# Root of the second layer's first norm: ScalarE's square root and VectorE's reciprocal, or one power on GpSimd

## The chip, the cores and the metric

The kernel runs on one core of a Trainium2 chip. The metric is the device time of one execution in microseconds (us), from the first to the last instruction with what lies around them; the median of the runs is what is compared. Engines are named as in the profile: PE (TensorE; PEld its weight loads), DVE (VectorE), ACT (ScalarE), POOL (GpSimd), SP (the queue that issues most transfers).

## The reference, cut to what matters

A two-layer model over 16 sequences of 548 tokens (36 from image patches, 512 from a word table) of 64 channels. The first layer is an attention with ReLU and a top-1 mixture of 8 experts with limited places; the second is a linear attention over 16 heads and a top-2 mixture of 8 experts. The part at stake is the norm ahead of the second layer's attention:

```python
def _layernorm(x, axis=-1, eps=1e-05):
    m = jnp.mean(x, axis=axis, keepdims=True)
    v = jnp.var(x, axis=axis, keepdims=True)
    return (x - m) / jnp.sqrt(v + eps)
...
h = h + _L0_ffn_ref(_layernorm(h, axis=-1), ...)      # first layer's experts
h = h + _L1_attn_ref(_layernorm(h, axis=-1), ...)     # the norm that is changed
h = h + _L1_ffn_ref(_layernorm(h, axis=-1), ...)      # second layer's experts
```

## The kernel before, in words

A sequence ("block" b, 0 to 15) is held as 128 partitions x 5 slots x 64 channels in `H[:, b]`. The kernel has two phases. Phase one runs the first layer for all blocks up to the scatter of the tokens to their experts, and then the first layer's experts in 24 units. Phase two, the functions `pool_second`, `pe_second`, `act_second` and `dve_second`, takes each block through: fetching the expert outputs (`gather_first`, 3 indirect transfers, and `gather_rest`, 2, both issued by POOL, L382), weighting and cleaning them (`scale`, `limits`, `mask`; on DVE inside `mixed` for the first BY_DVE = 3 blocks, on POOL from block 3 on), adding them to H (`mixed`, L650 and L652), the norm's statistics (`mixed_stats`: five `bn_stats` of L1354 and five `bn_aggr` of L1357), the root (`roots4`, ACT, L548), the norm itself (`norm4`, DVE, L670 to L673), PE's turn of it (`t4`, L977), ACT's copy of that (`stack4`, L566), keys and values (`kv`, L990), their bias (`kv_b`, DVE, L680), the norm of keys and values (`square`, `sum_squares`, `roots_kv`, `kvnorm`), the small products `gram` to `by_proj` (L447 to L472), `proj` (L990), its GELU on ACT (`gelu_proj`, L578), the second residual and its statistics (`resid2`, `resid2_stats`), two roots (`roots5`, L559 and L560), `norm5`, `route` (L496) and the choice of two experts. In that choice `second_share` (POOL, L412) raises a 128x5 tile of Euler numbers to a power. Then come the second layer's experts: for each block 8 units of two `up` halves (PE, L1012 and L1013), two GELUs (ACT, L607), a `down` (PE, L521), a `weigh` (DVE, L852) and a `summed` (POOL, L422).

Each engine runs its instructions in order. The order is set by hand: every function has a time in a table (`POOL_TWO`, `PE_TWO`, `ACT_TWO`, `DVE_TWO`), block b's is 32 later for each block, and `in_order` sorts each engine's list by these times. Engines are tied together by semaphores alone, so a function that waits holds all that stands behind it on its engine. On DVE the order around the norm is `mixed` 43, `mixed_stats` 45, `norm4` 67; `mixed` of the next block (75) comes after `norm4` of this one. On POOL, in units of the same scale, `gather_first` of block b+2 stands at 46.75, `gather_rest` of block b+2 at 54.75. Steps inside a function count up a semaphore (`Steps`, `PER` gives their number); `sync` waits until all those issued so far have ended.

The square root and the GELU lie in different function tables of ACT. A change of table is an instruction of its own (ACT_TABLE_LOAD) ahead of the first activation that needs the other table; in the profile it has the line of that activation. The changed places are `PER` (L53), `POOL_TWO` (L250), `ACT_TWO` (L254), `pool_second` (L369), `act_second` (L544 to L548), `mixed_stats` (L654) and `norm4` (L662).

Of the kernel before, what the change touches and what calls it, by code (L numbers as in the profile page):

```python
# [9 lines left out]
ALU = mybir.AluOpType  # L10
ACT = mybir.ActivationFunctionType
# [3 lines left out]
P = 128  # L15
NB, N_IMG, N_TXT, D = 16, 36, 512, 64
N = N_IMG + N_TXT
SLOTS = 5
# [12 lines left out]
EPS = 1e-5  # L31
# [19 lines left out]


PER = dict(norm1a=11, norm1b=4, qk_low=3, vals=1, resid=1, norm2a=11, norm2b=5, norm3a=10, norm3b=3, gate=6, place=7,  # L53
           mixed=12, weighted=5, norm4=3, kvnorm=3, fold=3, resid2=11, norm5=5, route_a=10, route_b=6)


class Steps:
# [43 lines left out]
def units(middle, lag, name, step=1):  # L101
    return [(middle + (n + lag) * PERIOD / POS, name, n) for n in range(step - 1, NB * POS, step)]
# [17 lines left out]
def early_fusion_kernel(nc, i, out):  # L120
    with ExitStack() as ctx:
        def sb(name, shape, dt=F32):
            return ctx.enter_context(nc.sbuf_tensor(name, shape, dt))

        def pair(name, shape, dt=F32, depth=2):
            return [sb(f"{name}{k}", shape, dt) for k in range(depth)]
# [3 lines left out]
        def sem(name):  # L130
            if name not in sems:
                sems[name] = ctx.enter_context(nc.semaphore(name))
            return sems[name]
# [27 lines left out]
        eps_t = sb("eps_t", [P, 2])  # L161
# [14 lines left out]
        stats = sb("stats", [P, SLOTS, 6])  # L176
        mv1, mv2, mv3 = (pair(f"mv{k}_", [P, SLOTS, 2]) for k in (1, 2, 3))
        sd1 = pair("sd1_", [P, 2, SLOTS])
        sd2, sd3 = pair("sd2_", [P, SLOTS]), pair("sd3_", [P, SLOTS])
        rs = sb("rs", [P, 2, SLOTS])  # L180
        zt = sb("zt", [P, SLOTS, D])
# [29 lines left out]
        def bc(a, n):  # L211
            return a.unsqueeze(2).to_broadcast([a.shape[0], a.shape[1], n])
# [13 lines left out]
        def at(s):  # L226
# [20 lines left out]
                   (227, "norm2b"), (233, "norm3a"), (255, "norm3b"), (267, "gate"), (280, "place"))  # L247
        MOE, SQUEEZE_TWO, DOWN_LAG, GELU_LAG, WEIGH_LAG, SUM_LAG = 171.5, {}, 1.25, 0.5, 2.5, 0
        B_START, B_STEP, B_READY = -34.5, 2.7, -60
        POOL_TWO = ((-17.25, "gather_first"), (-9.25, "gather_rest"), (1.5, "scale"), (10.75, "limits"), (25.75, "mask"), (97.5, "input_added"),  # L250
                    (141, "second_share"))
        PE_TWO = ((75.25, "t4"), (77.5, "kv"), (95.5, "gram"), (97.75, "gains_k"), (100, "gains_v"), (101.5, "by_q"), (104.25, "by_proj"),
                  (114.75, "proj"), (131.5, "t5_even"), (134.5, "t5_odd"), (135.75, "route"), (160, "t8"), (220.5, "back"))
        ACT_TWO = ((70.25, "roots4"), (76.25, "stack4"), (81.75, "square"), (90, "roots_kv"), (117.5, "gelu_proj"), (122.5, "roots5"),  # L254
                   (126.25, "high5"), (135.5, "stack5_even"), (136.25, "stack5_odd"), (162.5, "copy_w8"))
        DVE_TWO = ((43, "mixed"), (45, "mixed_stats"), (67, "norm4"), (82, "kv_b"), (82.5, "sum_squares"), (89.75, "kvnorm_inv"), (90.25, "kvnorm"),
                   (92.5, "gram_s"), (96.75, "p1_s"), (97.5, "own_heads"), (98.5, "add_input"), (106, "fold"), (114.75, "pre_bias"),
# [38 lines left out]
        x4 = xt  # L296
# [13 lines left out]
        euler = sb("euler", [P, SLOTS])  # L310

        def unit(n):
            return divmod(n, POS)
# [54 lines left out]

        def pool_second(pool):  # L369
            pool.memset(euler[:], 2.718281828459045).then_inc(sem("euler"), 1)  # L370
            pool.wait_ge(sem("euler"), 1)
            pool.wait_ge(sem("norm2a"), NB * PER["norm2a"])
            pool.wait_ge(sem("norm2b"), NB * PER["norm2b"])

            def gather_y(b, slots):
                if b <= 1 and slots[0] == 0:
                    stored(pool, (FIRST_UNITS, NU)[b])
                if b >= 2 and slots[0] == 0:
                    pool.wait_ge(sem("mixed"), (b - 2) * PER["mixed"] + 1)
                for s in slots:  # L380
                    rows = P if s < TXT else N_IMG
                    pool.indirect_dma_start(yg[b % 2][0:rows, s, :], None, expert_out, bass.IndirectOffsetOnAxis(slot_i[0:rows, b, (s + 1) % SLOTS:(s + 1) % SLOTS + 1], 0),  # L382
                                            bounds_check=E * CP - 1, oob_is_err=False).then_inc(sem(f"y_in{b % 2}"), 16)

            def gather_first(b):
                gather_y(b, (0, 1, 2))

            def gather_rest(b):
                gather_y(b, (3, 4))

            def scale(b):
                if b >= BY_DVE:
                    weighted_scale(pool, b)

            def limits(b):
                if b >= BY_DVE:
                    weighted_limits(pool, b)

            def mask(b):
                if b >= BY_DVE:  # L400
                    weighted_mask(pool, b)

            def input_added(b):
                pool.wait_ge(sem("norm4"), (b + 1) * PER["norm4"])
                pool.tensor_tensor(H[:, b], H[:, b], x4[b % 2][:, 0:SLOTS, :], ALU.add).then_inc(sem("input_added"), 1)

            def second_share(b):

                pool.wait_ge(sem("route_a"), (b + 1) * PER["route_a"])
                if b >= 1:  # L410
                    pool.wait_ge(sem("route_b"), b * PER["route_b"])
                pool.tensor_tensor(ex[:], euler[:], mx[:], ALU.pow).then_inc(sem("share"), 1)  # L412

            def summed(n):
                b, e = unit(n)
                if e == 0:
                    return
                pool.wait_ge(sem("weigh"), n + 1)
                m = b * (POS - 1) + e
                if e >= 2:  # L420
                    pool.wait_ge(sem("summed"), m - 1)
                pool.tensor_tensor(total[b % 2][:, 0:RIGHT], total[b % 2][:, 0:RIGHT], part[m % PARTS], ALU.add).then_inc(sem("summed"), 1)  # L422

            table = dict(gather_first=gather_first, gather_rest=gather_rest, scale=scale, limits=limits, mask=mask, input_added=input_added, second_share=second_share, summed=summed)
            for name, b in in_order(POOL_TWO, MOE, SQUEEZE_TWO, units(MOE, SUM_LAG, "summed")):
                table[name](b)

# [113 lines left out]
                table[name](b)  # L541

        def act_second(act, first_experts):
            def roots4(b):  # L544
                act.wait_ge(sem("mixed"), (b + 1) * PER["mixed"])
                if b >= 2:
                    act.wait_ge(sem("norm4"), (b - 2) * PER["norm4"] + 1)
                act.activation(sd2[b % 2][:], mv1[b % 2][:, :, 1], ACT.Sqrt, bias=eps_t[:, 0:1]).then_inc(sem("roots4"), 1)  # L548

            def roots_kv(b):  # L550

                act.wait_ge(sem("ssq"), b + 1)
# [63 lines left out]
                    act.wait_ge(sem("share_out"), 16 * (b - 1))  # L616
                act.activation(w8t[b % 2], bank(1)[0:E * SLOTS, 0:P], ACT.Identity).then_inc(sem("w8t"), 1)

            table = dict(first_experts, roots4=roots4, roots_kv=roots_kv, roots5=roots5, stack4=stack4, square=square, gelu_proj=gelu_proj, stack5_even=stack5_even, stack5_odd=stack5_odd, high5=high5, copy_w8=copy_w8, gelu=gelu)
            for name, b in in_order(ACT_TWO, MOE, SQUEEZE_TWO, units(MOE, GELU_LAG, "gelu") + expert_units(B_START, B_STEP, NU, ((0, "b_stack"), (1.5, "b_relu")))):  # L620
                table[name](b)

        def dve_second(dve, first_experts):
# [30 lines left out]
            def mixed_stats(b):  # L654
                st = Steps(dve, sem("mixed"), "mixed", b, 2)
                shared.take(dve, ("stats",), sem("mixed"), (b + 1) * PER["mixed"])
                if b >= 2:
                    dve.wait_ge(sem("norm4"), (b - 1) * PER["norm4"])
                norm_stats(dve, st, H[:, b], mv1[b % 2])
                st.close()  # L660

            def norm4(b):  # L662
                st = Steps(dve, sem("norm4"), "norm4", b)
                shared.take(dve, ("rs", "zt"), sem("norm4"), (b + 1) * PER["norm4"])
                dve.wait_ge(sem("roots4"), b + 1)
                dve.wait_ge(sem("mixed"), (b + 1) * PER["mixed"])
                if b >= 2:
                    dve.wait_ge(sem("t4"), b - 1)
                    dve.wait_ge(sem("input_added"), b - 1)
                st(dve.reciprocal(rs[:, 0, :], sd2[b % 2][:]))  # L670
                st(dve.tensor_tensor(zt[:], H[:, b], bc(mv1[b % 2][:, :, 0], D), ALU.subtract))
                st.sync()
                st(dve.tensor_tensor(x4[b % 2][:, 0:SLOTS, :], zt[:], bc(rs[:, 0, :], D), ALU.mult))  # L673
                st.close()

            def kv_b(b):
# [206 lines left out]
        def stored(engine, count):  # L883
            for k in range(YO):
                engine.wait_ge(sem(f"expert_out{k}"), 16 * len(range(k, count, YO)))
# [87 lines left out]
        shared = Banks()  # L973
# [377 lines left out]
        def norm_stats(dve, st, src, mv):  # L1351

            for s in range(SLOTS):
                st(dve.bn_stats(stats[:, s, :], src[:, s, :]))  # L1354
            st.sync()
            for s in range(SLOTS):
                st(dve.bn_aggr(mv[:, s, :], stats[:, s, :]))  # L1357
# [352 lines left out]
```

## Time and profile before

| | us |
|---|---|
| median of 3 runs (lowest, highest) | 857.36 (856.84, 860.45) |
| the profiled execution | 856.15 |
| its span, first to last instruction | 854.3 |
| busy: PE, DVE, ACT, POOL | 727.0, 586.5, 490.5, 436.5 |

The first layer ends at about 359 us of the span. From about 360 to 430 us the second layer starts up block by block; from about 430 us on, its experts run and one block takes about 27 us, with the front of block b beside the experts of block b-4. Times in the rows are us from the start of the span. A row of a timeline gives start, duration, engine, line, operation, tiles and shapes, the number of instructions that were merged, and in brackets the engine's idle time before it and who ended that.

### The profile page before, as it was taken

The numbers are of one execution on the slowest core, as the hardware profiler recorded it, in microseconds if no ns is written. First come the engines' busy times: TensorE is split into PE (matmuls) and PEld (weight loads), VectorE is DVE, ScalarE is ACT, GpSimd is POOL, SyncE is SP. The second block draws the span as 40 slices with busy tenths as digits, with TensorE's granted clock in tenths as the row PEclk, the third lists the DMA queues.
The fourth block names the chain that finished last, engine by engine and source line by source line (L and its number), as shares of the span: only waits on it lengthen the run. The fifth ranks groups of instructions, "written<-read, shape, count | busy, mean of one in ns | idle before, by whom it ended". The sixth has DMA issues, their size and how long they took to land.

```text
span 854.3 us, 16008 instructions
## 1 busy us (share of the span) xinstructions
PE 727.0 (85%) x4863; PEld 542.2 (63%) x4863; DVE 586.5 (69%) x2216; ACT 490.5 (57%) x923; POOL 436.5 (51%) x457
## 2 busy tenths in 40 slices
PE   4599999999973399735599999999999999999994
PEld 3467777777752266524377776677767777777773
DVE  2658898998886255656777777877778777765421
ACT  1356656565622266403377777667866678775652
POOL 4743547783655400265647666576666754223321
PEclk9599999999975599955589999999999999999998
DMA  8900000000000122200112321122202222022220
GB/s 244 362 15 11 9 15 22 22 19 3 5 4 3 45 87 88 62 20 8 24 37 55 62 62 33 31 62 63 62 16 49 62 63 60 10 54 62 62 61 13
DMA packets 49534, 43.69 MB, mean 51 GB/s; under 512 B 19962, under 2 KB 45066, under 8 KB 49066
## 3 DMA queue, kind: packets, MB, share of 16 engines
q1 hardware_dynamic: 40666, 36.33, 16.6%
q0 software_dynamic: 7200, 4.17, 2.2%
q10 hardware_dynamic: 1584, 2.18, 0.8%
q8 instruction: 40, 0.66, 0.3%
q14 instruction: 44, 0.36, 0.1%
HBM read 31.65 MB, written 13.47 MB: 53 GB/s over the span
## 4 chain that ended last, share of the span: by engine, by line
PE 45%; DVE 14%; ACT 9%; issue 7%; DMA 0%; DVEq 0%; POOL 0%; POOLq 0%; ACTq 0%
PE psum L521 9%; PE psum L1012 8%; PE psum L1013 6%; ACT scratch L607 3%; PE psum L1199 3%; PE psum L496 2%; PE psum L990 2%; ACT L607 2%; ACT L553 2%; PE psum L983 2%; PE psum L447 2%; DVE stats L1354 2%; PE psum L1181 1%; DVE xt L680 1%; DVE mv L1357 1%
## 5 line engine op out<-in xcount | busy, mean ns | idle before, releaser
L607 ACT ACTIVATE scratch<-psum,fb 128x584 f32<-128x584 f32 x256 | 177.3, 744 | 97.8 <-PE psum L1013 95.7
L422 POOL TENSOR_TENSOR prob<-prob,scratch 128x292 f32<-128x292 f32 x112 | 81.2, 725 | 150.1 <-DVE scratch L852 145.4
L521 PE MATMUL psum<-scratch,w_fw 128*64 128x292 f32 (+1 forms) x1024 | 143.0, 401 | 0.1
L382 POOL DMA_INDIRECT uu<-expert_out,slot_i x80 | 82.9, 1036 | 86.6 <-issue 77.0
L1012 PE MATMUL psum<-kh,fw_hi 128*128 128x292 f32 x352 | 105.7, 323 | 10.8 <-ACT scratch L607 10.7
L943 POOL DMA_INDIRECT slots_buf<-xt,slot_i x80 | 81.8, 1022 | 57.6 <-DVE slot_i L1594 36.0
L521 PEld LDWEIGHTS psum<-scratch,w_fw 128*64 128x64 f32 x1024 | 89.4, 136 | 27.6 <-DVE scratch L852 5.2
L1013 PE MATMUL psum<-kh,fw_lo 128*128 128x292 f32 x352 | 93.0, 291 | 0.0
L929 POOL DMA_INDIRECT emb<-in_table,w_ids x64 | 63.0, 984 | 54.3 <-DVE stats L1354 33.2
L1012 PEld LDWEIGHTS psum<-kh,fw_hi 128*128 128x128 f32 x352 | 66.8, 190 | 27.3 <-ACT scratch L607 16.0
L1256 ACT ACTIVATE prob<-psum 128x292 f32<-128x292 f32 (+1 forms) x160 | 54.9, 396 | 30.5 <-PE psum L1066 30.5
L852 DVE SCALAR_TENSOR_TENSOR scratch<-psum,w_fb,X 128x292 f32<-128x292 f32 x112 | 55.1, 512 | 18.9 <-PE psum L521 18.5
L1013 PEld LDWEIGHTS psum<-kh,fw_lo 128*128 128x128 f32 x352 | 67.1, 191 | 0.0
L1065 PE MATMUL psum<-qst,kh 128*128 128x292 f32 (+1 forms) x160 | 53.8, 351 | 0.1
L1012 PE MATMUL psum<-kl,fw_hi 128*128 128x292 f32 (+1 forms) x160 | 47.7, 321 | 4.5 <-ACT scratch L607 4.5
L1075 PE MATMUL psum<-prob,vv 128*64 128x256 f32 (+1 forms) x320 | 50.3, 408 | 0.5 <-ACT prob L1256 0.5
L1354 DVE BATCH_NORM_STATS2 stats<-H 128x6 f32<-128x64 f32 x320 | 46.7, 212 | 1.8 <-DVE H L1519 0.5
L977 PE MATMUL psum<-w_ident,xt 128*128 128x128 f32 x144 | 27.9, 308 | 20.4 <-DVE xt L1544 8.8
L1066 PE MATMUL psum<-qst,kl 128*128 128x292 f32 (+1 forms) x160 | 43.1, 290 | 0.0
L1013 PE MATMUL psum<-kl,fw_lo 128*128 128x292 f32 (+1 forms) x160 | 42.0, 290 | 0.0
L1012 PEld LDWEIGHTS psum<-kl,fw_hi 128*128 128x128 f32 x160 | 30.1, 188 | 12.0 <-ACT scratch L607 7.0
L1357 DVE BATCH_NORM_AGGREGATE mv<-stats 128x2 f32<-128x6 f32 x400 | 35.6, 156 | 2.8
(262 smaller groups left out, 1696.1 us busy)
## 6 DMA issues: line engine op xcount, KB each, us to landing
X<-share_buf SPq DMA_DIRECT2D x16, 584.0 KB, 5.9
X<-share_buf SPq DMA_DIRECT2D x16, 512.0 KB, 7.7
slots_buf<-zeros SPq DMA_DIRECT2D x8, 352.0 KB, 4.4
expert_out<-zeros SPq DMA_DIRECT2D x8, 352.0 KB, 4.2
X<-slots_buf SPq DMA_DIRECT2D x16, 128.0 KB, 2.0
expert_out<-X SPq DMA_DIRECT2D x16, 128.0 KB, 1.7
out<-H SPq DMA_DIRECT2D x16, 128.0 KB
X<-in_patches ACTq DMA_DIRECT2D x1, 1728.0 KB, 7.0
```

What stands on the lines that cost most here:

```text
L382: pool.indirect_dma_start(yg[b % 2][0:rows, s, :], None, expert_out, bass.IndirectOffsetOnAxis(slot_i[0:rows, b, (s + 1) % SLOTS:(s + 1) % ...
L422: pool.tensor_tensor(total[b % 2][:, 0:RIGHT], total[b % 2][:, 0:RIGHT], part[m % PARTS], ALU.add).then_inc(sem("summed"), 1)
L521: last = pe.matmul(bank(6 + n % 2)[h * D:(h + 1) * D, 0:z], w["fw2"][:, e * J + j, :], hid[(J * n + j) % (J * UNITS)][:, h, 0:z], start=(j ...
L607: act.activation(hid[(J * n + j) % (J * UNITS)], both(2 + 2 * j), ACT.Gelu, bias=fb1[:, e * J + j:e * J + j + 1]).then_inc(sem("gelu"), 1)
L852: dve.scalar_tensor_tensor(out=dst, in0=bank(6 + n % 2)[:, 0:RIGHT], scalar=w["fb2"][:, e:e + 1], in1=share[b % 2][:, e, :], op0=ALU.add, ...
L929: pool.indirect_dma_start(emb[b % 2][:, t, :], None, i["table"], bass.IndirectOffsetOnAxis(w["ids"][:, b * TXT + t:b * TXT + t + 1], 0)).t ...
L943: pool.indirect_dma_start(slots_buf, bass.IndirectOffsetOnAxis(slot_i[0:rows, b, (s + 1) % SLOTS:(s + 1) % SLOTS + 1], 0), xt3[b % XT3][0: ...
L1012: pe.matmul(dst, parts[0][:, cols], rhs, start=True, stop=False)
L1013: return pe.matmul(dst, parts[1][:, cols], rhs, start=False, stop=True)
L1065: pe.matmul(dst, kh[b % 2][:, at(s):at(s) + P], q_side, start=True, stop=False)
L1256: act.activation(prob[s][:, FIRST[h]:FIRST[h] + z], bank(SCORE[h])[:, 0:z], ACT.Relu, scale=SCALE).then_inc(sem("relu"), 1)
L1354: st(dve.bn_stats(stats[:, s, :], src[:, s, :]))
```

## The change

The root of the variance is no longer taken by ACT. DVE adds epsilon to the five variances (a new last step of `mixed_stats`, after a `sync`, on a 128x5 tile), POOL raises the sum to the power -0.5 in a function `roots4` of its own, and `norm4` multiplies by that: its reciprocal and its use of the shared tile `rs` are gone. `roots4` leaves ACT's list (it stood at 70.25) and enters POOL's at 52, so behind `gather_first` of block b+2 and ahead of `gather_rest` of block b+2. POOL sets the exponents once by a memset.

```diff
-           mixed=12, weighted=5, norm4=3, ...
+           mixed=13, weighted=5, norm4=2, ...
+        var4, rs4, minus_half = pair("var4_", [P, SLOTS]), pair("rs4_", [P, SLOTS]), sb("minus_half", [P, SLOTS])
-        POOL_TWO = ((-17.25, "gather_first"), (-9.25, "gather_rest"), (1.5, "scale"), ...
+        POOL_TWO = ((52, "roots4"), (-17.25, "gather_first"), (-9.25, "gather_rest"), (1.5, "scale"), ...
-        ACT_TWO = ((70.25, "roots4"), (76.25, "stack4"), ...
+        ACT_TWO = ((76.25, "stack4"), ...
         def pool_second(pool):
             pool.memset(euler[:], 2.718281828459045).then_inc(sem("euler"), 1)
-            pool.wait_ge(sem("euler"), 1)
+            pool.memset(minus_half[:], -0.5).then_inc(sem("euler"), 1)
+            pool.wait_ge(sem("euler"), 2)
+
+            def roots4(b):
+                pool.wait_ge(sem("mixed"), (b + 1) * PER["mixed"])
+                if b >= 2:
+                    pool.wait_ge(sem("norm4"), (b - 1) * PER["norm4"])
+                pool.tensor_tensor(rs4[b % 2][:], var4[b % 2][:], minus_half[:], ALU.pow).then_inc(sem("roots4"), 1)
...
         def act_second(act, first_experts):
-            def roots4(b):
-                act.wait_ge(sem("mixed"), (b + 1) * PER["mixed"])
-                if b >= 2:
-                    act.wait_ge(sem("norm4"), (b - 2) * PER["norm4"] + 1)
-                act.activation(sd2[b % 2][:], mv1[b % 2][:, :, 1], ACT.Sqrt, bias=eps_t[:, 0:1]).then_inc(sem("roots4"), 1)
...
             def mixed_stats(b):
...
                 norm_stats(dve, st, H[:, b], mv1[b % 2])
+                st.sync()
+                st(dve.tensor_scalar(var4[b % 2][:], mv1[b % 2][:, :, 1], EPS, None, ALU.add))
                 st.close()

             def norm4(b):
                 st = Steps(dve, sem("norm4"), "norm4", b)
-                shared.take(dve, ("rs", "zt"), sem("norm4"), (b + 1) * PER["norm4"])
+                shared.take(dve, ("zt",), sem("norm4"), (b + 1) * PER["norm4"])
                 dve.wait_ge(sem("roots4"), b + 1)
                 dve.wait_ge(sem("mixed"), (b + 1) * PER["mixed"])
...
-                st(dve.reciprocal(rs[:, 0, :], sd2[b % 2][:]))
                 st(dve.tensor_tensor(zt[:], H[:, b], bc(mv1[b % 2][:, :, 0], D), ALU.subtract))
                 st.sync()
-                st(dve.tensor_tensor(x4[b % 2][:, 0:SLOTS, :], zt[:], bc(rs[:, 0, :], D), ALU.mult))
+                st(dve.tensor_tensor(x4[b % 2][:, 0:SLOTS, :], zt[:], bc(rs4[b % 2][:], D), ALU.mult))
                 st.close()
```

## Rows read from the trace of the kernel before

**Rows 1.** Busy time by stretch: the start-up of the second layer.

```profile
360.00:430.00 70.00, 34.23 (x142) 23.89 (x143) 45.98 (x171) 15.51 (x31) 40.21 (x38) 0.50 0.12 27
```

**Rows 2.** Busy time by stretch: ten periods of one block, 430 to 700.5 us, sum.

```profile
sum 270.50, PE 255.53 PEld 195.90 DVE 204.02 ACT 201.21 POOL 176.16; mean PE 25.55 PEld 19.59 DVE 20.40 ACT 20.12 POOL 17.62
```

**Rows 3.** Waits of PE, 430 to 840 us: total us, times, longest.

```profile
PE psum L1012 <- ACT scratch L607: 15.3, 35, 1.2
PE psum L990 <- DVE xt L680: 4.2, 11, 0.7
```

**Rows 4.** Timeline of PE, one period (560 to 590 us).

```profile
569.32 0.94 PE L990 MATMUL psum<-emb,ot 128*128 128x128 f32 x6 [0.28 <-DVE xt L680]
...
579.87 0.40 PE L1012 MATMUL psum<-kl,fw_hi 128*128 128x292 f32 x1 [0.52 <-ACT scratch L607]
```

**Rows 5.** Timeline of DVE, the same period.

```profile
562.42 0.20 DVE L792 TENSOR_TENSOR lg<-psum,ratio 128x40 f32<-128x40 f32 x1 [0.31 <-PE psum L496]
...
564.29 0.51 DVE L650 COPY_PREDICATED prob<-rr,uu 128x320 f32<-128x320 int32 x1
...
566.13 0.45 DVE L1357 BATCH_NORM_AGGREGATE mv<-stats 128x2 f32<-128x6 f32 x5
566.50 0.24 DVE L803 SCALAR_TENSOR_TENSOR eq<-lg,w_order 128x40 f32<-128x40 f32 x1
...
568.45 0.81 DVE L680 TENSOR_TENSOR xt<-psum,w_kv_b 128x640 f32<-128x640 f32 x1
...
574.60 0.17 DVE L822 TENSOR_SCALAR qq<-ex 128x5 f32<-128x5 f32 x1
...
586.99 0.19 DVE L670 RECIPROCAL rs<-sd 128x5 f32<-128x5 f32 x1
```

**Rows 6.** Groups of ACT's instructions by line, whole span.

```profile
L548 ACT ACT_TABLE_LOAD x13 | 16.7, 1283 | 0.2
```

**Rows 7.** Timeline of ACT, the same period.

```profile
568.57 1.39 ACT L607 ACTIVATE scratch<-psum,fb 128x584 f32<-128x584 f32 x2 [3.33 <-PE psum L1013]
...
584.73 1.28 ACT L548 ACT_TABLE_LOAD   x1
586.03 0.30 ACT L548 ACTIVATE sd<-mv,eps_t 128x5 f32<-128x5 f32 x1
```

**Rows 8.** Timeline of POOL, the same period.

```profile
561.30 0.87 POOL L339 TENSOR_TENSOR prob<-prob 128x320 f32<-128x320 f32 x1
...
572.58 1.21 POOL L412 TENSOR_TENSOR ex<-euler,mx 128x5 f32<-128x5 f32 x1
...
582.78 0.89 POOL L422 TENSOR_TENSOR prob<-prob,scratch 128x292 f32<-128x292 f32 x1 [4.26 <-DVE scratch L852]
```

**Rows 9.** Timeline of POOL, start of the second layer.

```profile
368.26 1.03 POOL L382 DMA_INDIRECT uu<-expert_out,slot_i  x1 [0.30 <-issue]
...
371.21 1.22 POOL L382 DMA_INDIRECT uu<-expert_out,slot_i  x1 [0.30 <-issue]
```

**Rows 10.** Timeline of DVE, start of the second layer.

```profile
363.93 0.19 DVE L670 RECIPROCAL rs<-sd 128x5 f32<-128x5 f32 x1 [0.42 <-ACT sd L548]
364.03 0.45 DVE L671 TENSOR_TENSOR zt<-H,mv 128x320 f32<-128x320 f32 x1
364.51 0.49 DVE L673 TENSOR_TENSOR xt<-zt,rs 128x320 f32<-128x320 f32 x1
369.54 0.49 DVE L327 TENSOR_TENSOR uu<-uu,top_w 128x320 f32<-128x320 f32 x1 [4.53 <-DMA uu<-expert_out,slot_i]
...
373.79 0.79 DVE L680 TENSOR_TENSOR xt<-psum,w_kv_b 128x640 f32<-128x640 f32 x1
```

**Rows 11.** Timeline of PE, start of the second layer.

```profile
366.62 2.62 PE L990 MATMUL psum<-w_wkv,ot 128*128 128x256 f32 x6 [0.59 <-ACT ot L566]
```

**Rows 12.** Timeline of ACT, start of the second layer.

```profile
374.62 0.74 ACT L572 ACTIVATE xt<-xt 128x640 f32<-128x640 f32 x1 [8.14 <-DVE xt L680]
376.24 0.34 ACT L553 ACTIVATE prob<-prob 128x160 f32<-128x160 f32 x1 [0.89 <-DVE prob L686]
```

More of the change, by code:

```diff
@@ L53 @@
 PER = dict(norm1a=11, norm1b=4, qk_low=3, vals=1, resid=1, norm2a=11, norm2b=5, norm3a=10, norm3b=3, gate=6, place=7,
-           mixed=12, weighted=5, norm4=3, kvnorm=3, fold=3, resid2=11, norm5=5, route_a=10, route_b=6)
+           mixed=13, weighted=5, norm4=2, kvnorm=3, fold=3, resid2=11, norm5=5, route_a=10, route_b=6)
 class Steps:
@@ L249, in early_fusion_kernel @@
         B_START, B_STEP, B_READY = -34.5, 2.7, -60
-        POOL_TWO = ((-17.25, "gather_first"), (-9.25, "gather_rest"), (1.5, "scale"), (10.75, "limits"), (25.75, "mask"), (97.5, "input_added"),
+        POOL_TWO = ((52, "roots4"), (-17.25, "gather_first"), (-9.25, "gather_rest"), (1.5, "scale"), (10.75, "limits"), (25.75, "mask"), (97.5, "input_added"),
                     (141, "second_share"))
@@ L253, in early_fusion_kernel @@
                   (114.75, "proj"), (131.5, "t5_even"), (134.5, "t5_odd"), (135.75, "route"), (160, "t8"), (220.5, "back"))
-        ACT_TWO = ((70.25, "roots4"), (76.25, "stack4"), (81.75, "square"), (90, "roots_kv"), (117.5, "gelu_proj"), (122.5, "roots5"),
+        ACT_TWO = ((76.25, "stack4"), (81.75, "square"), (90, "roots_kv"), (117.5, "gelu_proj"), (122.5, "roots5"),
                    (126.25, "high5"), (135.5, "stack5_even"), (136.25, "stack5_odd"), (162.5, "copy_w8"))
@@ L422, in summed @@
                 pool.tensor_tensor(total[b % 2][:, 0:RIGHT], total[b % 2][:, 0:RIGHT], part[m % PARTS], ALU.add).then_inc(sem("summed"), 1)
-            table = dict(gather_first=gather_first, gather_rest=gather_rest, scale=scale, limits=limits, mask=mask, input_added=input_added, second_share=second_share, summed=summed)
+            table = dict(roots4=roots4, gather_first=gather_first, gather_rest=gather_rest, scale=scale, limits=limits, mask=mask, input_added=input_added, second_share=second_share, summed=summed)
             for name, b in in_order(POOL_TWO, MOE, SQUEEZE_TWO, units(MOE, SUM_LAG, "summed")):
@@ L617, in copy_w8 @@
                 act.activation(w8t[b % 2], bank(1)[0:E * SLOTS, 0:P], ACT.Identity).then_inc(sem("w8t"), 1)
-            table = dict(first_experts, roots4=roots4, roots_kv=roots_kv, roots5=roots5, stack4=stack4, square=square, gelu_proj=gelu_proj, stack5_even=stack5_even, stack5_odd=stack5_odd, high5=high5, copy_w8=copy_w8, gelu=gelu)
+            table = dict(first_experts, roots_kv=roots_kv, roots5=roots5, stack4=stack4, square=square, gelu_proj=gelu_proj, stack5_even=stack5_even, stack5_odd=stack5_odd, high5=high5, copy_w8=copy_w8, gelu=gelu)
             for name, b in in_order(ACT_TWO, MOE, SQUEEZE_TWO, units(MOE, GELU_LAG, "gelu") + expert_units(B_START, B_STEP, NU, ((0, "b_stack"), (1.5, "b_relu")))):
```

## The prediction

> **What bounds the kernel now.** I read the busy time by stretch first. From 430 us on, one block takes 27.05 us (270.5 over ten), and in it PE is busy 25.55, DVE 20.4, ACT 20.1 and POOL 17.6 us [rows 2]. So PE is the bound there, and its few gaps are what a change can win or lose. The waits of PE name them: 15.3 us for ACT's GELUs (35 times), and 4.2 us for the bias of keys and values, once in each of 11 blocks [rows 3]. The start-up before that is another stage: from 360 to 430 us PE is busy 34 of 70 us, its granted clock is 0.50 (1.2 GHz), and DVE with 46 us is the busiest [rows 1]. There blocks 0 to 3 go through a serial chain of small steps, and any delay of one step is a delay of the end.
>
> Then the timelines around the change, in both stages. In the period at 562 us DVE starts the routing step when PE's route is done (0.31 us idle, released by PE) and then works without a hole through `mixed`, the statistics and the choice of expert to `kv_b` at 568.45, and PE's `proj` at 569.32 waits for that, 0.28 us [rows 4, 5]. What lengthens DVE between 562.4 and 568.5 lands on PE. POOL raises a 128x5 tile to a power in 1.21 us [rows 8], the very shape of the new root.
>
> **The change part by part.**
>
> *ACT, removed.* A root of 0.30 us, and in 13 of the 16 blocks the table load of 1.28 us ahead of it [rows 6, 7]; the GELU behind it needs a load back of the same length. Steady state: 2 x 1.28 + 0.30 = 2.9 us less of ACT per block, some 37 us over 13 blocks. What hides it today: in the same period ACT stands idle 3.33 us at 568.57, waiting for PE [rows 7], after it has caught up from the root at 584.7 of the period before; and PE's wait for a GELU is at 579.87, ahead of the root [rows 4]. Time freed behind 584.7 makes that idle stretch longer and reaches no wait of PE. I take 0.
>
> The Trainium skill, "ScalarE: Activation LUTs", section "What ACT_TABLE_LOAD costs", charges a drain of about 1.38 us beside the load, 2.66 us per change of table. The trace doesn't show the drain here: the load starts at 584.73, takes 1.28 and the root starts at 586.03. By the page ACT would be rid of some 36 us more; my sum would stay as it is, since ACT isn't the bound, but the faster rival below would gain weight.
>
> *ACT, the first load.* Block 0's load is hidden today, since ACT waits for the statistics anyway. Without `roots4` the first root in the second layer is `roots_kv`, behind the square at 374.62 + 0.74 = 375.36. A load there ends at 376.64 + 0.02; the root starts today at 376.24 [rows 12]. Loss 0.4 us, on the start-up chain. Bounds: 0 if the load lands earlier, 1.3 if it starts only when the root is ready.
>
> *DVE, removed.* The reciprocal takes 0.19 us, but the subtraction starts 0.10 behind it [rows 10], so 0.10 us. In steady state it lies ahead of DVE's wait for the route (0.31 idle [rows 5]): no gain.
>
> *DVE, added.* One 128x5 addition, 0.17 us for the same shape (L822) [rows 5], after a sync. A step behind a sync starts 0.03 after the end of the one before (364.03 + 0.45, then 364.51 [rows 10]), while today the next step starts 0.08 ahead of the end of the last `bn_aggr` (566.13 + 0.45 = 566.58 against 566.50 [rows 5]). With the same overlap behind the addition that step starts at 566.58 + 0.03 + 0.17 - 0.08 = 566.70, so +0.20 us per block. It sits inside the stretch that `proj` waits for. 11 blocks in steady state: 2.2 us. In the start-up it is between the statistics and `kv_b` for blocks 1 to 3: 0.6 us. Together 2.8. Bounds 0 (a slack I overlook) and 0.35 each (sync and addition in full, 14 x 0.35 = 4.9).
>
> *POOL, added, steady state.* 1.21 us behind the sum that ends at 582.78 + 0.89 = 583.67 [rows 8]: from 583.7 to 584.9. `norm4` starts at 586.99 [rows 5], so the result is 2.1 us early. Behind it stand `gather_rest`, one sum and `mask`, all 1.2 us later. The mask ends at 562.17 today and DVE uses it at 564.29 [rows 5, 8]: 2.1 us of slack, 0.9 left. Then POOL waits for DVE again. Cost 0. If the slack were gone, each further us would stall DVE inside the stretch above.
>
> *POOL, added, block 0.* Here the place in POOL's list decides. `roots4` of block 0 stands behind the three issues of `gather_first` of block 2, and those behind the five of block 1, which waited for the stores of the first layer's experts. Today the root comes from idle ACT, and `norm4` of block 0 starts at 363.93 [rows 10]. In the new order POOL is free for it only after the issue that starts at 371.21 and takes 1.22 [rows 9], so at 372.43; some of these issues ran slower beside DVE's work, which will now wait too, so rather 368.26 + 2 x 1.33 + 1.03 = 371.95. Plus 1.21: the root is there at 373.2. `norm4` (0.48 + 0.49 without the reciprocal) then ends at 374.2. On DVE's list the next is `mixed` of block 1, which starts today at 369.54, when its data land [rows 10]. It would start at 374.1: 4.5 us late. PE's side: `kv` ends today at 366.62 + 2.62 = 369.24, at the end of a turn and a copy that start when `norm4` ends, at 364.51 + 0.49 = 365.0 [rows 10, 11]; it moves by 374.2 - 365.0 = 9.2 us to 378.4, and `kv_b`, today at 373.79, moves to 373.79 + 4.5 + 0.2 = 378.5. So the slack there just covers it. Head loss 4.5 us; the stretch behind it is serial, so I expect all of it at the end. Bounds: 3.3 (a power as short as a root of 0.3 us on ACT, with the issues unhindered) and 5.5 (issues as slow as now and some lag).
>
> For blocks 1 to 3 POOL has waited for DVE before its gathers and `norm4` comes late behind the small products; no loss. The second memset falls where POOL is idle.
>
> *Sum.* 4.5 + 0.4 + 2.8 = 7.7 us. Against the profiled execution: 856.15 + 7.7 = 863.9. The median of the runs is 1.2 us above that execution, so 857.36 + 7.7 = **865.1 us**, 0.9% slower. What a measurement of this kernel can tell from no change is about 0.5%, 4.3 us: below 853.1 is faster, above 861.7 slower.
>
> **The rivals.**
>
> *Head only* (0.10). DVE's addition is hidden, because the weighing or PE's `kv` is the later release of `kv_b`. For it: only 0.28 us of wait. Against it: DVE shows no hole before it. 857.4 + 4.9 = 862.3.
>
> *Steady only* (0.08). The late root of block 0 is caught up in the start-up, as in 360 to 430 us DVE is busy only 46 of 70 us [rows 1]. Against it: the chain passes DVE, PE and ACT in turn. 857.4 + 0.4 + 2.8 = 860.6.
>
> *ACT's relief decides* (0.06, faster). PE's 15.3 us of waits for GELUs [rows 3] shrink because ACT enters each round of GELUs earlier. It decides where ACT has no idle time between the root and such a wait; at 568.57 it has 3.33 us [rows 7]. All of it gained against 7.7 lost: 857.4 + 7.7 - 15.3 = 849.8. The page's rule, to batch activations by table, points this way.
>
> *POOL is too slow* (0.05, slower still). The 0.9 us left to the mask is used up, say by 1 us per block over 11 blocks: 865.1 + 11 = 876.
>
> *It changes nothing* (0.04). The root arrives at block 0 in time after all and the addition is free, 857.4. For that POOL's issues would have to be much shorter than the rows show.
>
> **How the numbers follow.** The forecast has 0.67. Its own range takes low bounds 3.3 + 0 + 1.5 (half the addition) and high bounds 5.5 + 1.3 + 4.9: 862.2 to 869.1. PE's clock returns to full level only in the experts' stage, and later relative to the work it could cost or give back about a us. I widen the range to hold the two rivals just below: 860.0 to 869.0; some 0.18 is left outside. Slower by over 0.5%: the forecast, POOL's rival and most of head only, 0.77. Within 0.5%: steady only, nothing, and the low edge, 0.17. Faster: 0.06.
>
> **What the changed profile would show.** L548's 13 loads gone, and 13 of L607's with them. `roots4` of block 0 on POOL starting at about 372, `norm4` of block 0 at about 373 instead of 363.9, and DVE idle for some 9 us between. `mixed` of block 1 at 374. A load ahead of `roots_kv` at 375 + 4.7. The period from 430 us on longer by 0.2 us, PE's wait for L680 up from 4.2 to 6.5 us, its wait for L607 still near 15. I am wrong if `norm4` of block 0 stays near 364, if the block period doesn't grow, or if PE's waits for L607 fall by over 3 us.

## The result, and the profile after

The change made the kernel slower: 870.62 us median of 4 runs (868.34 to 872.85) against 857.87 (856.84 to 860.45), a ratio of 1.0144 with a 95% interval of 1.0109 to 1.0179. That is 12.8 us, where 7.7 were forecast, and 1.6 us above the upper end of the range.

The page of the changed kernel, busy times (the profiled execution took 872.85 us, its span is 871.0):

```profile
span 871.0 us, 15987 instructions
PE 727.1 (83%) x4863; PEld 541.8 (62%) x4863; DVE 599.4 (69%) x2216; ACT 456.1 (52%) x883; POOL 462.7 (53%) x474
```

PE does the same work in a longer span. ACT lost 34.4 us of work, POOL gained 26.2, and DVE, which should have gained a few us, is busy 12.9 us more. The time went where DVE is busy longer. PE's waits from 430 to 857 us:

```profile
PE psum L1015 <- ACT scratch L609: 15.4, 35, 1.2
PE psum L993 <- DVE xt L683: 11.2, 11, 1.3
```

These are the lines of [rows 3]. The wait for ACT's GELUs is 15.4 us after 15.3: ACT's relief shortened none of it. The wait for `kv_b` grew from 4.2 to 11.2 us in the same 11 blocks, 0.64 us each, three times the 0.20 forecast.

Two executions differ by some us in the first layer, which the change doesn't touch, so I split the second layer by five moments: the first `mixed` (start of its predicated copy in block 0), the `kv_b` of blocks 0, 3 and 15, and the end of the span. The start of DVE's instruction counts. Before, then after:

```profile
361.19 0.51 DVE L650 COPY_PREDICATED prob<-rr,uu 128x320 f32<-128x320 int32 x1
432.92 0.82 DVE L680 TENSOR_TENSOR xt<-psum,w_kv_b 128x640 f32<-128x640 f32 x1
756.76 0.82 DVE L680 TENSOR_TENSOR xt<-psum,w_kv_b 128x640 f32<-128x640 f32 x1 [0.86 <-PE psum L990]
```

```profile
364.24 0.52 DVE L652 COPY_PREDICATED prob<-rr,uu 128x320 f32<-128x320 int32 x1
...
381.62 0.82 DVE L683 TENSOR_TENSOR xt<-psum,w_kv_b 128x640 f32<-128x640 f32 x1
442.38 0.83 DVE L683 TENSOR_TENSOR xt<-psum,w_kv_b 128x640 f32<-128x640 f32 x1 [0.55 <-PE psum L993]
773.48 0.82 DVE L683 TENSOR_TENSOR xt<-psum,w_kv_b 128x640 f32<-128x640 f32 x1 [0.86 <-PE psum L993]
```

With 373.79 for block 0 before [rows 10] this gives the first two lines of a table that the experiments continue. "Head" is from the first `mixed` to `kv_b` of block 0, "start-up" from there to block 3, "steady" the 12 periods from block 3 to block 15.

| kernel | head | start-up | steady | rest | sum |
|---|---|---|---|---|---|
| before | 12.60 | 59.13 | 323.84 | 97.5 | 493.1 |
| after | 17.38 | 60.76 | 331.10 | 97.5 | 506.8 |
| difference | +4.8 | +1.6 | +7.3 | 0 | +13.7 |

The head, on POOL and DVE of the changed kernel:

```profile
371.30 1.03 POOL L390 DMA_INDIRECT uu<-expert_out,slot_i  x1 [0.30 <-issue]
372.64 1.00 POOL L390 DMA_INDIRECT uu<-expert_out,slot_i  x1 [0.30 <-issue]
373.94 1.00 POOL L390 DMA_INDIRECT uu<-expert_out,slot_i  x1 [0.30 <-issue]
374.96 1.23 POOL L379 TENSOR_TENSOR rs<-var,minus_half 128x5 f32<-128x5 f32 x1
```

```profile
366.58 0.17 DVE L663 TENSOR_SCALAR var<-mv 128x5 f32<-128x5 f32 x1
376.28 0.49 DVE L674 TENSOR_TENSOR zt<-H,mv 128x320 f32<-128x320 f32 x1 [9.52 <-POOL rs L379]
```

The sum of variance and epsilon is there at 366.75. POOL takes its power at 374.96, behind the gathers of block 2, and DVE stands idle for 9.52 us. Before, DVE waited 0.42 us at this place and then 4.53 for the gathered data [rows 10], so most of the wait was free.

In steady state the new thing is the length of DVE's instructions. DVE, then POOL, of one block of the changed kernel:

```profile
571.83 0.82 DVE L674 TENSOR_TENSOR zt<-H,mv 128x320 f32<-128x320 f32 x1
...
575.03 0.70 DVE L801 TENSOR_TENSOR lg<-lg,mx 128x40 f32<-128x40 f32 x1
...
576.29 0.52 DVE L652 COPY_PREDICATED prob<-rr,uu 128x320 f32<-128x320 int32 x1
576.84 0.84 DVE L654 TENSOR_TENSOR H<-H,prob 128x320 f32<-128x320 f32 x1
577.71 0.73 DVE L1357 BATCH_NORM_STATS2 stats<-H 128x6 f32<-128x64 f32 x5
578.48 0.45 DVE L1360 BATCH_NORM_AGGREGATE mv<-stats 128x2 f32<-128x6 f32 x5
578.96 0.72 DVE L663 TENSOR_SCALAR var<-mv 128x5 f32<-128x5 f32 x1
579.60 0.19 DVE L806 SCALAR_TENSOR_TENSOR eq<-lg,w_order 128x40 f32<-128x40 f32 x1
579.82 0.20 DVE L783 TENSOR_REDUCE qq<-eq 128x5 f32<-128x40 f32 x1
580.05 0.20 DVE L785 TENSOR_TENSOR oh<-eq,qq 128x40 f32<-128x40 f32 x1
```

```profile
568.48 1.21 POOL L379 TENSOR_TENSOR rs<-var,minus_half 128x5 f32<-128x5 f32 x1
...
574.80 0.87 POOL L340 TENSOR_TENSOR prob<-prob 128x320 f32<-128x320 f32 x1
575.63 1.70 POOL L430 TENSOR_TENSOR prob<-prob,scratch 128x292 f32<-128x292 f32 x2
578.12 0.72 POOL L328 TENSOR_TENSOR uu<-uu,top_w 128x320 f32<-128x320 f32 x1 [0.79 <-DVE stats L1357]
578.80 0.86 POOL L413 TENSOR_TENSOR H<-H,xt 128x320 f32<-128x320 f32 x1
```

The same steps in the kernel before, DVE, then POOL's pair of sums:

```profile
563.15 0.58 DVE L798 TENSOR_TENSOR lg<-lg,mx 128x40 f32<-128x40 f32 x1
...
564.84 0.49 DVE L652 TENSOR_TENSOR H<-H,prob 128x320 f32<-128x320 f32 x1
```

```profile
562.12 1.55 POOL L422 TENSOR_TENSOR prob<-prob,scratch 128x292 f32<-128x292 f32 x2
```

Read the ends of both in the changed kernel. The small L801 ends at 575.73, POOL's L340 at 575.67. The addition of epsilon, a 0.17 us instruction, starts at 578.96 and ends at 579.68; POOL's L413 ends at 579.66. The addition to H (L654) takes 0.84 us after 0.49, and POOL's pair of sums reaches to 577.33, into it; before the change that pair had ended at 563.67, 1.2 us before the addition. An operation of DVE that falls on one of POOL ends later, as if it could not run until POOL's ends. Others aren't touched: L783 takes 0.20 whatever POOL does.

This is no accident of one block. In the second layer of the traces of all twelve kernels (the two above and the ten below) 625 DVE steps that read two tensors from SBUF start while POOL is at a two-input step on 128x292 or 128x320 and that step has at least 0.2 us to go. 624 of them take longer than alone, and they end 0.05 to 0.06 us (128x40) or 0.34 to 0.38 us (128x320) behind POOL's end. Of 1345 steps that read at most one tensor from SBUF (statistics, reductions, and `kv_b`, whose other input is in PSUM) none takes longer. Beside a power of POOL (128x5, 1.2 us) none of 227 two-input steps does. So the new power itself holds nothing up; what matters is where POOL's large steps come to lie.

### The profile page after: what moved, and what is told of

It is laid out like the page before. It is cut to its first block, busy times and chain, and to the rows that moved or that the text cites. A ratio compares the mean times of both kernels' runs of the same rounds, so it can differ in the third digit from the quotient of the medians.

```text
span 871.0 us, 15987 instructions
## 1 busy us (share of the span) xinstructions
PE 727.1 (83%) x4863; PEld 541.8 (62%) x4863; DVE 599.4 (69%) x2216; ACT 456.1 (52%) x883; POOL 462.7 (53%) x474
## 4 chain that ended last, share of the span: by engine, by line
PE 29%; issue 15%; DVE 14%; POOL 12%; ACT 4%; POOLq 0%; DVEq 0%; DMA 0%; ACTq 0%
PE psum L529 5%; POOL uu L390 5%; PE psum L1015 5%; PE psum L1016 3%; PE psum L1202 3%; POOL prob L430 3%; ACT scratch L609 2%; DVE stats L1357 2%; POOL rr L338 2%; PE psum L1184 1%; PE psum L993 1%; DVE H L654 1%; DVE mv L1360 1%; POOL ex L420 1%; DVE scratch L855 1%
## 5 line engine op out<-in xcount | busy, mean ns | idle before, releaser
L430 POOL TENSOR_TENSOR prob<-prob,scratch 128x292 f32<-128x292 f32 x112 | 84.9, 758 | 151.1 <-DVE scratch L855 146.8
L946 POOL DMA_INDIRECT slots_buf<-xt,slot_i x80 | 81.7, 1022 | 59.1 <-DVE slot_i L1597 37.6
L980 PEld LDWEIGHTS psum<-w_ident,xt 128*128 128x128 f32 x144 | 19.0, 156 | 36.1 <-issue 31.1
```

The costliest lines, as they stand in the source:

```text
L946: pool.indirect_dma_start(slots_buf, bass.IndirectOffsetOnAxis(slot_i[0:rows, b, (s + 1) % SLOTS:(s + 1) % SLOTS + 1], 0), xt3[b % XT3][0: ...
```

## The experiments

I had three theories of the steady loss: half POOL's later work and half the addition (theory 1), the addition alone (2), POOL's place alone (3). All took the head for POOL's order. The first four kernels below ran on another chip, on which the kernel before takes 914.16 us; PE's granted clock over the first layer is 0.84 to 0.86 there in place of 0.89 to 0.90. In the steady stage it is 1.00 in these four traces as in the two above, and the last stage takes 97.4 to 97.6 us in every run, so I compare the stages with those of the kernel before in the table. Each stage figure is from one profiled execution.

### The power at 46

```diff
-        POOL_TWO = ((52, "roots4"), (-17.25, "gather_first"), ...
+        POOL_TWO = ((46, "roots4"), (-17.25, "gather_first"), ...
```

> The changed kernel with POOL's power at 46 in place of 52, that is ahead of gather_first of block b+2. Theory 1 (the start is lost to POOL's order; in the steady state about half of the loss is POOL's later work holding DVE, half is DVE's addition): kv_b of block 0 about 1.2 us behind the kernel before in place of 4.8; the block period from kv_b of block 4 to 15 longer by 0.3 us in place of 0.66; total about +5.5 us against the kernel before. Theory 2 (the steady loss is the addition alone): period +0.66 as in the changed kernel, total about +9.5. Theory 3 (the steady loss is POOL's place alone): period +0, total about +2.

Ratio to before 1.0001 (0.997 to 1.0031). Head 13.5, start-up 61.2, steady 323.4, sum 495.6 us: of the 13.7 us lost, 2.5 are left. Theory 1 said +5.5, theory 2 +9.5, theory 3 +2, which is the nearest. Nothing was taken away, one instruction was moved in POOL's list, ahead of three transfer issues and two sums. Its timeline in steady state:

```profile
607.65 1.20 POOL L420 TENSOR_TENSOR ex<-euler,mx 128x5 f32<-128x5 f32 x1
608.84 1.17 POOL L379 TENSOR_TENSOR rs<-var,minus_half 128x5 f32<-128x5 f32 x1
...
614.00 0.72 POOL L430 TENSOR_TENSOR prob<-prob,scratch 128x292 f32<-128x292 f32 x1
617.83 0.88 POOL L430 TENSOR_TENSOR prob<-prob,scratch 128x292 f32<-128x292 f32 x1 [3.11 <-DVE scratch L855]
```

The power stands ahead of a hole of POOL, which shrinks from 4.26 [rows 8] to 3.11 us and gives POOL its old timing back. At 52 it stood behind that hole and pushed all that follows. The addition to H takes 0.49 us again in every steady block.

### One unused power at 52 in the kernel before

```diff
-        POOL_TWO = ((-17.25, "gather_first"), ...
+        POOL_TWO = ((52, "spare_power"), (-17.25, "gather_first"), ...
...
+            def spare_power(b):
+                if b >= 1:
+                    pool.wait_ge(sem("spare_power"), b)
+                pool.tensor_tensor(rs4[:], euler[:], minus_half[:], ALU.pow).then_inc(sem("spare_power"), 1)
...
```

> The kernel before plus one unused power of 128x5 on POOL per block at 52, for which nobody waits. Theory 1: period +0.35 us, no loss at the start, total about +4. Theory 2: no change. Theory 3: period +0.66, total about +7.

Ratio 1.0055 (1.0025 to 1.0085). Head 12.5, start-up 59.7, steady 329.6, sum 499.3: +5.7 us over the 12 periods, 0.48 each, between theories 1 and 3. Nobody waits for this power; its whole price is what it pushes:

```profile
621.52 0.84 DVE L659 TENSOR_TENSOR H<-H,prob 128x320 f32<-128x320 f32 x1
```

```profile
619.48 0.87 POOL L340 TENSOR_TENSOR prob<-prob 128x320 f32<-128x320 f32 x1
620.31 1.70 POOL L429 TENSOR_TENSOR prob<-prob,scratch 128x292 f32<-128x292 f32 x2
```

The same 0.84 us for the addition to H, with the same pair of sums beside it, in 10 of the 12 periods: 3.5 us. The rest of the 5.7 I have not split. The choice's subtraction (128x40) is held longer too, 1.5 us in all, and so is `norm4`, whose last step takes 0.87 us in place of 0.49; most of that goes into DVE's wait for the route, which falls from 4.3 us over the 12 periods to 0.5.

### The addition alone

```diff
...
+                st.sync()
+                st(dve.tensor_scalar(var4[b % 2][:], mv1[b % 2][:, :, 1], EPS, None, ALU.add))
...
-                act.activation(sd2[b % 2][:], mv1[b % 2][:, :, 1], ACT.Sqrt, bias=eps_t[:, 0:1]).then_inc(sem("roots4"), 1)
+                act.activation(sd2[b % 2][:], var4[b % 2][:], ACT.Sqrt).then_inc(sem("roots4"), 1)
```

> The kernel before with epsilon added by DVE behind the statistics, and ACT's root taken of that sum. Theory 1: period +0.3 us, total about +4. Theory 2: period +0.66, total +7 to +8. Theory 3: no change.

Ratio 1.0001 (0.9961 to 1.0041). Steady 324.6, +0.7 us over 12 periods; theory 2 is out. Start-up 60.9, +1.8 us; 1.3 of it lie between the `kv_b` of blocks 0 and 1, against 0.9 in the changed kernel, which has the load there as well. I didn't follow that up.

```profile
626.20 0.23 DVE L662 TENSOR_SCALAR var<-mv 128x5 f32<-128x5 f32 x1
626.34 0.18 DVE L806 SCALAR_TENSOR_TENSOR eq<-lg,w_order 128x40 f32<-128x40 f32 x1
626.56 0.20 DVE L783 TENSOR_REDUCE qq<-eq 128x5 f32<-128x40 f32 x1
626.79 0.52 DVE L785 TENSOR_TENSOR oh<-eq,qq 128x40 f32<-128x40 f32 x1
```

In this block the addition is nearly free of POOL, and L785, at the end of the little chain, pays the wait for POOL. It paid it in the kernel before as well, with 0.55 us. In eight of the last 11 blocks the addition takes 0.17 to 0.29 us here, in the other three up to 0.46. In the changed kernel its median over these blocks is 0.50 us, up to 0.72: it pays at the head of the chain, and the three steps behind it come on top.

### No root on ACT

The root is replaced by a copy of the variance, so the norm is left without its root.

```diff
-                act.activation(sd2[b % 2][:], mv1[b % 2][:, :, 1], ACT.Sqrt, bias=eps_t[:, 0:1]).then_inc(sem("roots4"), 1)
+                act.activation(sd2[b % 2][:], mv1[b % 2][:, :, 1], ACT.Identity, bias=eps_t[:, 0:1]).then_inc(sem("roots4"), 1)
```

> The kernel before with ACT's root of the second layer's first norm replaced by a copy of the variance (the root is left out), which needs no table: ACT is rid of the table loads around it, and nothing is added anywhere. Theories 1 to 3: -0.2 to +0.5 us (the first load may now lie ahead of the root of keys and values). Rival (ACT's relief is worth something): up to 15 us faster.

Ratio 1.0013 (0.9982 to 1.0044), which tells nothing finer. By stages: steady 323.2, so 0.6 us in 12 periods is all that 24 table loads less (31 us) are worth here. The start-up takes 60.2 after 59.1, and 0.6 of that lie between the `kv_b` of blocks 0 and 1, where the first load now is:

```profile
437.09 0.74 ACT L572 ACTIVATE xt<-xt 128x640 f32<-128x640 f32 x1 [8.42 <-issue]
437.84 1.28 ACT L553 ACT_TABLE_LOAD   x1
439.14 0.34 ACT L553 ACTIVATE prob<-prob 128x160 f32<-128x160 f32 x1
```

The root starts 1.31 us behind the square in place of 0.88 [rows 12], 0.43 us late.

### The unused power at 46

The kernel before with the unused power, as above, but at 46.

```diff
-        POOL_TWO = ((-17.25, "gather_first"), ...
+        POOL_TWO = ((46, "spare_power"), (-17.25, "gather_first"), ...
...
```

> The kernel before plus the unused power on POOL, now at 46. Place theory (the power costs only where it pushes POOL's sum and mask into DVE's additions): block period as before, within 0.05 us, total 0 to +0.5. Amount theory (1.2 us more of POOL per block costs wherever it stands): +0.5 us per block as at 52, total about +6.

857.82 against 858.34 us, ratio 0.9987 (0.9975 to 0.9999). Head 12.8, start-up 60.1, steady 323.4, sum 493.9. In steady state the same instruction costs 5.7 us at 52 and nothing at 46: the amount theory is out. The start-up is 1.0 us longer all the same, with no load and no addition in it; below, that is PE's clock.

### The power at 46, the addition at 51.2

```diff
-        POOL_TWO = ((52, "roots4"), (-17.25, "gather_first"), ...
+        POOL_TWO = ((46, "roots4"), (-17.25, "gather_first"), ...
-        DVE_TWO = ((43, "mixed"), (45, "mixed_stats"), (67, "norm4"), ...
+        DVE_TWO = ((43, "mixed"), (45, "mixed_stats"), (51.2, "add_eps"), (67, "norm4"), ...
...
                 norm_stats(dve, st, H[:, b], mv1[b % 2])
-                st.sync()
+
+            def add_eps(b):
+                st = Steps(dve, sem("mixed"), "mixed", b, 12)
                 st(dve.tensor_scalar(var4[b % 2][:], mv1[b % 2][:, :, 1], EPS, None, ALU.add))
...
```

> The changed kernel with the power at 46 and DVE's addition as a step of its own at 51.2, in the hole ahead of resid2. Place theory: steady period 0.05 to 0.1 us below the kernel before (what ACT's relief gave in the run without the root), start as in the run at 46 or 0.2 better; from the first mixed to the end +1.5 to +2.3 us. If the addition costs wherever it stands: as the run at 46, +2.5.

858.36 against 858.34 us, ratio 1.0007 (0.9993 to 1.002). Head 13.4, start-up 60.4, steady 322.2, sum 493.5. The steady stage is now 1.6 us shorter than in the kernel before. The head (0.8) and the start-up (1.2, of which 0.4 lie where the first load is) take it back.

### Block 0 at 46, all others at 52

```diff
-        POOL_TWO = ((52, "roots4"), (-17.25, "gather_first"), ...
+        POOL_TWO = ((-17.25, "gather_first"), ...
...
-            for name, b in in_order(POOL_TWO, MOE, SQUEEZE_TWO, units(MOE, SUM_LAG, "summed")):
+            for name, b in in_order(POOL_TWO, MOE, SQUEEZE_TWO, units(MOE, SUM_LAG, "summed") + [(52 + b * PERIOD if b else 46, "roots4", b) for b in range(NB)]):
```

> The changed kernel with the power of block 0 alone at 46, all others at 52. If start and steady state add up: kv_b of block 0 only 0.9 us late behind the first mixed (4.8 in the changed kernel), the steady period still 0.6 us longer; from the first mixed to the end about +9.7 us in place of +13.6. If the steady loss follows from the late start: +2.5 or so.

One execution, 867.36 us. Head 13.5, start-up 61.1, steady 331.2, sum 503.3, +10.2. One place in POOL's list, for one block, is worth 3.9 us of head, and the steady loss stays. Head and steady loss are two things and add up.

### Two unused powers at 52

The kernel of the unused power at 52 with a second one behind it.

```diff
...
+                pool.wait_ge(sem("spare_power"), 2 * b + 1)
+                pool.tensor_tensor(rs4[:], euler[:], minus_half[:], ALU.pow).then_inc(sem("spare_power"), 1)
```

> The kernel before with two unused powers at 52 in place of one, which cost 0.5 us per block. Place theory: 1.2 us more use up what slack the mask has (it ended 0.9 us ahead of DVE's use by the prediction) and hold more of DVE's work, +1.0 to +1.6 us per block. If POOL's lag is absorbed by its waits: +0.5 as with one.

One execution, 882.01 us. Steady 348.6, +24.8 us, 2.1 per block against 0.5 for one: more than the upper end I gave. But 10.8 us of that are PE's clock. PE now waits 1.6 to 1.9 us for `kv_b` in ten blocks (at most 1.3 in the changed kernel), and behind six of these waits its granted clock falls from 1.00 to 0.50 (1.2 GHz), five times for 3.4 us and once for 6.8 (the stretch below, cut to a tenth of a us, gives 0.51). In no other trace does it fall in the steady stage. One of the waits, then the stretch behind it (busy time of PE, PEld, DVE, ACT and POOL, granted clock, DMA share, GB/s):

```profile
581.96 1.05 PE L999 MATMUL psum<-emb,ot 128*128 128x128 f32 x6 [1.86 <-DVE xt L689]
```

```profile
582.60:586.00 3.40, 3.40 (x16) 2.67 (x17) 1.45 (x4) 1.65 (x4) 3.24 (x3) 0.51 0.00 0
```

A period without a fall takes 28.5 us, one with a fall 30.0 to 30.1, the one with the long fall 31.5. With these extras taken off, two powers cost 14.0 us in the 12 periods, 1.2 per block and inside what I expected, and the second adds 0.7 per block, less than its own 1.2. DVE, then POOL:

```profile
576.12 0.95 DVE L659 COPY_PREDICATED prob<-rr,uu 128x320 f32<-128x320 int32 x1 [1.03 <-issue]
577.11 0.84 DVE L661 TENSOR_TENSOR H<-H,prob 128x320 f32<-128x320 f32 x1
```

```profile
575.17 0.86 POOL L340 TENSOR_TENSOR prob<-prob 128x320 f32<-128x320 f32 x1
575.99 1.61 POOL L431 TENSOR_TENSOR prob<-prob,scratch 128x292 f32<-128x292 f32 x2
```

Now the mask itself is late. It ends at 576.03 and the copy that needs it starts at 576.12, after DVE has stood idle for 1.03 us; the profile names no releaser there, so that DVE idles for the mask is my reading of the two times. Then the copy falls on POOL's sums as well, 0.95 us after 0.51.

### The addition moved, the power still at 52

```diff
-        DVE_TWO = ((43, "mixed"), (45, "mixed_stats"), (67, "norm4"), ...
+        DVE_TWO = ((43, "mixed"), (45, "mixed_stats"), (51.2, "add_eps"), (67, "norm4"), ...
...
```

> The changed kernel with the power still at 52 and only the addition moved into the hole at 51.2. If the addition costs 0.18 us per block in the changed kernel because it is held by POOL's two-input operation: 12 periods of 328.9 us in place of 331.1 (kernel before 323.9). If all of the loss is POOL's later sum: 331.

One execution, 870.43 us. Steady 328.9, as expected, start-up 60.1. So the addition costs 2.2 us over 12 periods in the changed kernel and 0.7 in the kernel before. With the power at 46 it costs 1.1 (323.4 against 322.2 with both moved). The truth lies between theories 1 and 3: POOL's place 5.7 us, the addition 2.2.

### Block 0's root by ACT, the rest at 46

The kernel with both moved, but ACT takes the root of block 0 and DVE inverts it; POOL skips that block.

```diff
...
+            def root_first(b):
+                if b == 0:
+                    act.wait_ge(sem("mixed"), PER["mixed"])
+                    act.activation(sd2[0][:], var4[0][:], ACT.Sqrt).then_inc(sem("roots4"), 1)
...
+                if b == 0:
+                    dve.reciprocal(rs4[0][:], sd2[0][:]).then_inc(sem("first_root"), 1)
...
```

> As the run with both moved, but block 0's root is taken by ACT and inverted by DVE as before. If the start's remaining loss is POOL's order and the table load, both go: kv_b of block 0 at 12.6 to 12.8 us behind the first mixed, no load ahead of the first root of keys and values, and the steady gain of 1.6 us stays: from the first mixed to the end 491.6 us, 1.5 us (0.17%) faster than the kernel before. If POOL's power costs something at the start in any case: no gain.

857.97 against 858.68 us, ratio 0.9991 (0.9976 to 1.0006). Head 12.6, start-up 59.2, steady 323.0, sum 492.1: 1.0 us less than before by stages. Head and load are gone as expected; of the steady 1.6 only 0.9 came. Against the kernel before it stands at -0.7 us, where the changed kernel stood at +12.8, and it is not to be told from the kernel before.

## Why the prediction was wrong

**The steps that held.** The head was forecast at 4.5 us and measured 4.8. The first load was forecast at 0.4 us; the root it delays is 0.43 us late, and from block 0's `kv_b` to block 1's the two runs with the load and with the addition moved take 16.2 us in place of 15.8. ACT's relief, forecast at 0, is worth 0.6 to 1.2 us in steady state (0.6 in the run without a root, 0.7 between the unused power at 52 and the changed kernel with the addition moved, 1.2 between the unused power at 46 and the kernel with both moved). PE's wait for GELUs stayed at 15.4 us; the faster rival had no ground. The drain that the Trainium skill ("ScalarE: Activation LUTs", "What ACT_TABLE_LOAD costs") adds to a load does not show here either: in the run without a root the activation starts 0.02 us behind the end of the load.

**The step that failed** is "POOL, added, steady state ... Cost 0". I had checked who waits for POOL, and found the power 2.1 us early and the mask with 0.9 us left. In the block shown the power ends at 569.69 and `norm4` starts at 571.83, and the mask ends at 575.67, 0.62 us ahead of the copy that needs it. So nobody waits for either (it takes two powers to make the mask late). But an instruction of POOL can cost DVE time without any wait between them. It shifts POOL's later work along DVE's, and the pair of sums behind the mask, which my list of what moves did not even hold, came to lie across DVE's addition to H. The unused power at 52 prices this: 5.7 us in 12 periods. The same power at 46: nothing. That the shift is the cause is shown by these two runs, and that DVE's two-input steps wait for the end of POOL's by the 624 of 625 above.

The loss reaches PE through its wait for `kv_b`. Over the 12 periods, in us:

| kernel | PE's wait for `kv_b` | steady |
|---|---|---|
| both moved | 0.2 | 322.2 |
| unused power at 46 | 1.1 | 323.4 |
| before | 4.2 | 323.8 |
| unused power at 52 | 9.4 | 329.6 |
| changed | 11.2 | 331.1 |
| two unused powers at 52 | 18.5 | 348.6, of which 10.8 by the clock |

Which resource the two engines share no run can show. The Trainium skill states it: "SBUF — State Buffer", section "Who interferes with whom", says that DVE and GpSimd share a pair of ports as an exclusive lock, taken by DVE's instructions with two inputs in SBUF and by those in a two-port mode, which `tensor_scalar` can enter, and that `tensor_reduce` never contends on this chip. The rows agree: additions and the `tensor_scalar` are held, L783 is not. They differ in one thing: the section has such a DVE instruction contend with any GpSimd instruction that reads SBUF, and beside POOL's powers, which read two tiles there, none of 227 was held. The forecast had not weighed that page, and it would have changed the sum.

**The term that was right by luck.** The addition was forecast at 0.20 us per block, 2.2 us for 11, and the run with the addition moved says 2.2 for 12. But alone it costs 0.7, not 2.2. My working counted its duration and the sync; what it does is to decide which of DVE's small steps pays the wait for POOL. In the start-up the changed kernel lost 1.6 us; load and three additions make 1.0. The other 0.6 lie between the `kv_b` of blocks 2 and 3, and they go with PE's clock, of which the prediction had said that it "could cost or give back about a us". The granted clock, 0.50 (1.2 GHz) through the start-up, rises to 1.00 at 431.6 us before the change, 21.1 us behind block 2's `kv_b`; in the changed kernel 22.3 us behind it, and with the unused power at 46 24.1. The period takes 22.5, 23.1 and 23.5 us. What moves the rise I did not isolate, so differences of up to a us between start-ups above say nothing about load or addition.

**The sum.** Steady: 5.7 for the shift, 2.2 for the addition, 0.6 given back by ACT: 7.3, and 7.3 measured. That it closes to a tenth is luck in part, since ACT's share is anything from 0.6 to 1.2. With 4.8 and 1.6 it is 13.7 us by stages of the profiled executions; the medians give 12.8, and the first layer alone differs by 3 us between the two profiled executions. The rival "POOL is too slow" named the right engine, with a price of 1 us per block and a chance of 0.05. Its mechanism, a late mask, is what two powers show and not what one does.

## What to carry to other kernels

Before an instruction is given to GpSimd in a hand-made order, look for a hole of that engine and put the instruction ahead of it. A few places further, behind the hole, the same 1.2 us cost 0.5 us per block here. In the slack of GpSimd count not only who waits for it, but also which two-input operations of VectorE its later instructions will now lie beside. And follow the first pass of a loop by itself: the same place put block 0's root behind eight transfer issues, for 4.8 us, and moving it for that one block gave 3.9 back.

## What had not been expected of the hardware

One unused power on GpSimd cost 5.7 us in 12 periods and two cost 24.8, but 10.8 of these came by TensorE's clock: behind six of ten waits of 1.6 to 1.9 us it was granted 0.50 for 3.4 us or more, at about 1.5 us each (3.0 for the long one). A VectorE instruction of 0.17 us took 0.72 beside a GpSimd addition, and one of 0.49 took 0.84, while beside GpSimd's powers the same kinds of instruction took no longer than alone. And 34 us less work on ScalarE, 24 table loads among them, moved the end by about a us.
